# Attention probabilities transposed by DMA instead of by TensorE, in an eight-core block of attention and quantised FFN

## The reference

```
x = x + attn(layernorm(x))
x = x + ffn(layernorm(x))

attn: qkv = x @ w_qkv.T, reshaped to (N, 3, 16 heads, 128)
      att = softmax(einsum('bnid,bnjd->bnij', q, k) * 128**-0.5)
      out = einsum('bnij,bnjd->bnid', att, v)
      out.transpose(0, 2, 1, 3).reshape(B, N, 2048) @ w_proj.T
ffn:  fake_quant(relu(fake_quant(x) @ fake_quant(kernel) + fake_quant(bias)))
```

## Time and profile before

| | us |
|---|---|
| three runs, median (lowest, highest) | 635.04 (634.66, 636.46) |
| the profiled execution, its own time | 635.95 |
| span of its slowest core, core 5 | 634.3 |
| spans of the other cores | 631.6 to 633.4 |
| PE busy on core 5 | 606.1 (96%) |
| DVE / ACT busy on core 5 | 407.9 (64%) / 266.6 (42%) |

### The profile page before, as it was taken

The page is one execution under the profiler, slowest core; times in us unless marked ns, Lnnn a source line. Parts: engine busy times, 40 slices in busy tenths (PEclk is TensorE's granted clock), DMA queues, the critical chain, the costliest instruction groups (busy, mean ns, idle before and its releaser), DMA issues.

```text
span 634.3 us, 9870 instructions; the slowest of 8 cores (631.6 to 634.3 us)
## 1 busy us (share of the span) xinstructions
PE 606.1 (96%) x3468; PEld 304.6 (48%) x3468; DVE 407.9 (64%) x685; ACT 266.6 (42%) x491; POOL 34.7 (5%) x68
## 2 busy tenths in 40 slices
PE   6768999999999999999999999999999999999993
PEld 6634444444444444444444455555555444444442
DVE  3745888777778768761001346787787654888557
ACT  2763333443333344330010465767877422653331
POOL 0000100000100100001120000000000000000000
PEclk9999999999999999999999999999999999999998
DMA  8997899889999999758996672384433494062313
GB/s 236 261 217 221 139 237 219 174 190 195 190 230 185 228 232 194 177 102 150 154 157 102 120 168 78 101 246 121 133 94 61 157 285 136 30 196 106 102 66 133
DMA packets 54114, 103.48 MB, mean 163 GB/s; under 512 B 35633, under 2 KB 35633, under 8 KB 50225
## 3 DMA queue, kind: packets, MB, share of 16 engines
q0 software_dynamic: 9216, 33.56, 33.4%
q1 hardware_dynamic: 42674, 60.90, 31.7%
q10 hardware_dynamic: 2176, 8.39, 3.9%
HBM read 111.21 MB, written 16.79 MB: 202 GB/s over the span
## 4 chain that ended last, share of the span: by engine, by line
PE 89%; DMA 6%; DVE 2%; issue 1%; SPq 1%; ACT 1%; DVEq 0%; ACTq 0%
PE pF L832 50%; PE pF L937 17%; PE pF L914 17%; DMA xbuf<-x_att 6%; PE pF L871 1%; PE pF L895 1%; PE pH L881 1%; PE pF L872 1%; SPq L219 1%; PE pF L956 1%; PE pF L850 1%; DVE cols L514 0%; DVE xr L640 0%; DVEq L214 0%; DVE xr L807 0%
## 5 line engine op out<-in xcount | busy, mean ns | idle before, releaser
L832 PE MATMUL pF<-aT,wqb 128*128 128x512 bf16 x1504 | 327.1, 379 | 5.0 <-DMA wqb<-wqkv 5.0
L832 PEld LDWEIGHTS pF<-aT,wqb 128*128 128x128 bf16 x1504 | 146.4, 98 | 179.3 <-issue 5.4
L914 PE MATMUL pF<-wpq,qT 128*128 128x512 bf16 x512 | 119.6, 379 | 0.0
L937 PE MATMUL pF<-kq,xqT 128*128 128x512 bf16 x496 | 107.2, 379 | 1.2 <-DVE xr L640 1.2
L937 PEld LDWEIGHTS pF<-kq,xqT 128*128 128x128 bf16 x496 | 48.5, 98 | 59.9 <-issue 1.7
L914 PEld LDWEIGHTS pF<-wpq,qT 128*128 128x128 bf16 x512 | 47.8, 98 | 47.2
L385 ACT ACTIVATE wkz<-wkf 128x2048 f32<-128x2048 f32 x16 | 59.1, 3691 | 21.0 <-DVE wkf L607 21.0
L395 ACT ACTIVATE Ebuf<-pF,cols 128x128 bf16<-128x128 f32 x128 | 45.4, 368 | 24.6 <-DVE cols L621 24.5
L541 DVE CAST vT<-pF 128x512 bf16<-128x512 f32 x16 | 11.0, 689 | 62.7 <-PE pF L832 62.7
L685 DVE SCALAR_TENSOR_TENSOR tt<-pF,cols,bqb 128x512 f32<-128x512 f32 x31 | 23.2, 749 | 33.0 <-PE pF L937 33.0
L320 POOL DMA_DIRECT2D wqb<-wqkv x48 | 26.0, 543 | 298.7 <-PE pF L832 244.0
(11 more groups left out here) (79 smaller groups left out, 533.4 us busy)
## 6 DMA issues: line engine op xcount, KB each, us to landing
wqb<-wqkv POOLq DMA_DIRECT2D x48, 512.0 KB, 8.1
wkf<-wk SPq DMA_DIRECT2D x16, 1024.0 KB, 8.4
xbuf<-x_att SPq DMA_DIRECT2D x8, 1024.0 KB, 19.9
kq_spill<-kqr SPq DMA_DIRECT2D x16, 512.0 KB, 5.9
wpq<-wp POOLq DMA_DIRECT2D x16, 512.0 KB, 9.6
xr<-x_res ACTq DMA_DIRECT2D x8, 1024.0 KB, 6.7
kq<-kq_spill SPq DMA_DIRECT2D x4, 2048.0 KB, 11.1
out<-xr SPq DMA_DIRECT2D x7, 1024.0 KB, 4.2
```

Of the source, the lines that this page charges most:

```text
L832: mm = tn.matmul(pF[QBANK[j]][:, :], wqb[e % NW][:, 128 * c:128 * (c + 1)], aT[:, 8192 * h + 512 * c: 8192 * h + 512 * (c + 1)], start=(c ...
L914: mm = tn.matmul(pF[SLOTB[f % 3]][:, :], sT[:, 2048 * b + 128 * m: 2048 * b + 128 * (m + 1)], wpq[u][:, 512 * m:512 * (m + 1)], start=(m = ...
L937: mm = tn.matmul(pF[y % 4][:, :], xqT[:, 2048 * k + 128 * c: 2048 * k + 128 * (c + 1)], w[:, c, :, :], start=(c == 0), stop=(c == NC - 1))
```

## The change

The four PE transposes of each group and the ACT copy behind them are removed. In their place SP issues one transposing DMA per group, `e_transpose(g)`, from `Ebuf[g % 3]` to `aTT[g % 3]`; both have three buffers instead of two. It waits for `vNm` (the scaled probabilities) and for `av(g - 3)`, which has then read its `aTT`. `av(g)` waits for the DMA's semaphore `eT{g % 3}` instead of `sAT`, and `exps(g)` for the DMA of group g - 3 instead of the PE transpose of g - 2. Because SP works in order, its list is rewritten: the 32 new entries stand in the order of g, and `v_transpose`, `kq_load(0)` and `l_transpose(0..2)` are placed between them. The matmuls that warm PE up at the start read a tile of their own, `zero`, instead of `aTT[0]`.

```diff
     Ebuf = [A(f"Ebuf{i}", [128, 512], BF16, offset=204800 + 1024 * i)
-            for i in range(2)]
-    aTT = [A(f"aTT{i}", [128, 512], BF16, offset=206848 + 1024 * i)
-           for i in range(2)]
+            for i in range(3)]
+    aTT = [A(f"aTT{i}", [128, 512], BF16, offset=207872 + 1024 * i)
+           for i in range(3)]
+    zero = A("zero", [128, 128], BF16, offset=204800)
...
+            def e_transpose(g):
+
+                sync.wait_ge(S_("vNm"), g + 1)
+                if g >= 3:
+                    sync.wait_ge(S_("tO"), g - 2)
+                inc(sync.dma_start_transpose(
+                    aTT[g % 3].rearrange("p (j n) -> p j n", j=4),
+                    Ebuf[g % 3][:, :]), f"eT{g % 3}", 16)
...
-            for b in range(5):
-                v_transpose(b)
-            kq_load(0)
-            l_transpose(0)
-            v_transpose(5)
-            v_transpose(6)
-            l_transpose(1)
-            v_transpose(7)
-            l_transpose(2)
+            v_transpose(0)
+            v_transpose(1)
+            for g in range(NG):
+                e_transpose(g)
+                if g % 4 == 2 and 2 <= g // 4 + 1 < NT:
+                    v_transpose(g // 4 + 1)
+                if g == 8:
+                    kq_load(0)
+                if g in (17, 23, 29):
+                    l_transpose((g - 17) // 6)
...
             def exps(g):
                 s.wait_ge(S_("vMx"), g + 1)
-                if g >= 2:
-                    s.wait_ge(S_("tA"), g - 1)
+                if g >= 3:
+                    s.wait_ge(S_(f"eT{g % 3}"), 16 * (g // 3))
...
-                if 1 <= sl and sl - 1 < NG:
-                    att_evac(sl - 1)
...
             def av(g):
-                tn.wait_ge(S_("sAT"), g + 1)
+                tn.wait_ge(S_(f"eT{g % 3}"), 16 * (g // 3 + 1))
...
-                    if half == 0 and 1 <= sl <= NG:
-                        a_transp(sl - 1)
```

More of the change, by code:

```diff
@@ L390, in exps @@
                 s.wait_ge(S_("vMx"), g + 1)
-                if g >= 2:
-                    s.wait_ge(S_("tA"), g - 1)
+                if g >= 3:
+                    s.wait_ge(S_(f"eT{g % 3}"), 16 * (g // 3))
                 for j in range(4):
                     cs = slice(128 * j, 128 * (j + 1))
-                    i = s.activation(Ebuf[g % 2][:, cs], pF[3 + g % 2][:, cs],
+                    i = s.activation(Ebuf[g % 3][:, cs], pF[3 + g % 2][:, cs],
                                      AF.Exp, bias=cc(C_NM[g % 2] + j),
@@ L406, in xres_load @@
                         "p (h c) -> p h c", h=2)), f"xrL{b}", 16)
[L408 to L412, removed]
             def st_evac(g):
@@ L630, in a_norm @@
                 wt(v, h)
-                e3 = Ebuf[g % 2].rearrange("p (j n) -> p j n", j=4)
+                e3 = Ebuf[g % 3].rearrange("p (j n) -> p j n", j=4)
                 rb = cc(C_RD[g % 2], 4).unsqueeze(2).broadcast_to([128, 4, 128])
@@ L703, in _ @@
             inc(v.memset(cc(C_NMG), -MAGIC), "vNmg")
-            inc(v.memset(aTT[0][:, 0:128], 0.0), "vZ")
+            inc(v.memset(zero[:, :], 0.0), "vZ")
             stats(0)
@@ L896, in av @@
                                    V8[(g // 4) % 2][:, c0:c0 + 128],
-                                   aTT[g % 2][:, cs], start=True, stop=True)
+                                   aTT[g % 3][:, cs], start=True, stop=True)
                 inc(mm, "tO")
@@ L965, in warm @@
                 for i in range(n):
-                    tn.matmul(pF[5][:, 0:128], aTT[0][:, 0:128],
-                              aTT[0][:, 0:128], start=True, stop=True)
+                    tn.matmul(pF[5][:, 0:128], zero[:, :],
+                              zero[:, :], start=True, stop=True)
             tn.wait_ge(S_("vZ"), 1)
```

## The result

The changed kernel is slower: 648.81 us as the median of four runs (644.26 to 655.9) against 635.11 (634.66 to 636.46), a ratio of 1.018 (95% interval 1.012 to 1.024). Times are medians of all executions, while the ratios and their intervals leave out those in which half of the chip's cores ran at a lower clock, and those more than 1.5% over the kernel's fastest, which here is 655.9 and may be no more than this kernel's own scatter. The forecast was 628.3, with 626.8 to 632.5 as its range. The profiled execution took 644.26 us.

The account below looks back on a forecast made before the run. PE was taken to bound the kernel: 635.95 us profiled, less 7.2 for the transposes, plus 0.2 (group 9) and 0.3 (group 3), gives 629.25; against the runs' median the forecast is 628.3 us, range 626.8 to 632.5.

Parts of the forecast that it names:

- The removed work: Attention slots on PE: dropping four transposes saves 0.225 us per group, 7.2 us over 32 groups, giving slots of 4.12 us.
- The small DMA alone: One 128 x 512 transposing DMA, undisturbed: lands after 2.1 us (bounds 2.1 to 3.7) and holds SP 0.4 us.
- the moved steps: SP's list: v_transpose, l_transpose and the other moved entries cost nothing; v_transpose has 16 us of cover for a 3.7 us landing.
- sharing cost 3.2 us there: Core 1 transpose beside a residual load: landed after 6.9 us instead of 3.7, so a small one lands at 5.3, inside cover.
- group 3: Wait before av(3), its DMA beside a residual load and the wpq loads: taken as 0.3 us, bounds 0 to 1.5.
- `kq_load(0)` and group 9: Wait before av(9), its small DMA queued behind the 2 MB kq_load(0): taken as 0.2 us, bounds 0 to 1.7.
- late in more places: Rival: residual loads and v_transpose entries each delay one group past cover, three to five costing about 1 us; 630-633 us, chance 0.12.
- The slower rival: Rival: small transposes land as slowly as the slowest large ones in every slot, slower above 8.6 us; 637 or 674 us, chance 0.09.

Follow-up runs that it names:

- hybrid5_kq: Changed kernel with groups 0-4 transposed by PE, v_transpose(2..7) one group earlier, kq_load(0) behind group 31, l_transposes behind groups 19, 24, 29: 630.21 us, ratio 0.993.
- v_late: Kernel before the change, with v_transpose(2..7) made to wait so each starts within a microsecond of residual load b - 1: 634.87 us, ratio 1.001.
- v_early: Changed kernel with v_transpose(2..7) issued one group earlier on SP, residual loads still on ACT: 647.11 us, ratio 1.012.
- full_kq: Changed kernel, all 32 groups by DMA, with v_transpose one group earlier, kq_load(0) behind group 31, l_transposes behind groups 19, 24, 29: 639.74 us, ratio 1.007.
- no_wp: Changed kernel without POOL's last four wpq loads, zeros written instead: 641.37 us, ratio 1.010.
- xres_sp: Changed kernel with the eight residual loads issued by SP behind the transposing DMA of group 4b + 3, instead of by ACT: 636.94 us, ratio 1.004.

## Why the prediction was wrong

**The removed work: right.** 0.225 us a group and slots of 4.12 us are what the trace shows, and hybrid5_kq gives the whole sum back (27 x 0.223 us between the first and the last `av`). The Trainium skill's price for a PE transpose (TensorE: Matmul & The Clock Gate, Part 4: PE-mode transpose, about 275 ns) does not hold in this kernel as the cost of one: 108 transposes less gave 6.0 us, 56 ns each.

**The small DMA alone: right.** 2.3 us to land against 2.1. SP's 1.18 us against 0.4 was wrong by a factor of three and cost nothing, as hybrid5_kq shows.

**The step that failed is the moved steps.** The prediction priced `v_transpose(b)` by its cover only ("16 us of cover for 3.7 us") and said of all the moved entries "All of these cost nothing". It did not ask what else is on the DMA engines at the new moment. One group later on SP is the slot of the residual load, and the two start within 1 us of each other in 42 of 48 pairs. The new place alone does this: on core 7 group 10 is scaled at 402.90, its DMA issued at 403.03 and `v_transpose(3)` right behind it at 404.31, so `kq_load(0)` does not hold it up. That load, moved to group 8, was still under way (it landed at 406.0), and the transposes of this place are the slowest, 9.5 to 16.4 us against 7.7 to 11.3 elsewhere; that the third transfer is why is not shown.

The 3.7 us were a price from a place where the DMA engines were idle. v_late shows the collision by itself. v_early takes it away but at `v_transpose(3)`, which there does stand behind `kq_load(0)`, and hybrid5_kq and full_kq take that away too. Measured, this term is 7.2 us after `av(4)` as the mean of the cores and 10.6 on the worst, where the sum had 0.2 for group 9 and nothing else.

**The second failed term is "sharing cost 3.2 us there".** It came from one place, core 1, where I read the load's packets in the window as two transfers that ran side by side. They hardly did: the residual load was issued at 417.29, 7 us before the transpose (424.23); the transpose's first packet came at 426.37, and only the load's last 33 packets, up to 427.15, were left then.

Against an undisturbed transpose 1.0 of the 3.1 us lie before the first packet and 0.6 in the packets, which ran from 426.37 to 429.10; the last 1.5 lie between the last packet and the landing, when the load had landed (427.7), and what held it there is open. No row of the kernel before shows the two in each other's middle. A transpose that starts with a load takes 7.7 to 16.4 us, not 6.9.

The same row let group 3 pass as covered. That group was taken at 0.3 us, with a bound of 1.5 from loads that land when they did before, but they land later too (on core 7 the fourth `wpq` load after 14.0 us, where it took 8.7). Measured, groups 1 to 4 lost 3.6 to 8.4 us. no_wp shows that none of it comes without the `wpq` loads, and xres_sp that group 3's part goes too when residual load 0 leaves ACT's queue. I had also left groups 1 and 2 out, though the same `wpq` loads run beside them.

**`kq_load(0)` and group 9:** forecast 0 to 1.7 us at `av(9)`, measured 0.0 to 2.2 by core (core 7: 0.2). That term was nearly right in itself, and blind to what stands behind.

**The clock was not in the sum.** Behind the eight longest waits of the changed kernel (3.2 to 6.3 us) the slot has a granted clock of 0.63 to 0.74 on average, part of it at the lower level, and takes 1.4 to 2.3 us more than 4.12 (1.5 on core 7 behind the wait before `av(11)`). In v_early it is up to 2.9.

**The rivals.** The first one, "late in more places", was the right one in kind: it named residual loads and `v_transpose` entries. It was priced at 630 to 633, about 1 us a place, and refused with "6.9 us, for a DMA four times as large, is still under 7.9", the same row again. The lost time is 6.9 to 18.6 us by core. The slower rival needed a median landing over 8.6 us and was wrong: the median is 4.2, and no core's is higher than 4.4. I gave slower 0.09, because I asked only whether *every* group could be late and not whether a few could be very late.

## What to carry to other kernels

Where a DMA takes the place of an engine's work, price its landing beside what other queues move in that very microsecond, not from a row in which it ran alone, and do the same for each entry that is moved to make room. Small packets, transposing ones above all, should not start with another queue's load: put both on one queue, or keep them apart (a lead of 1.2 to 2.1 us was enough for the transpose here, 4.5 us and more in hybrid5_kq, where nothing is lost), or leave the work on the engine in the few slots where this can't be done. When each of many steps has its own cover, one late one costs its excess in full and the clock behind it, so sum over the worst places, and on the worst core, before the average.

## What the runs showed of the hardware

- A transposing DMA of 512 KB and a 1 MB load from memory on another queue, started within 1 us of each other, took 7.7 to 16.4 and 6.4 to 16.3 us in the changed kernel, and 8.0 to 11.5 and 7.4 to 10.9 in v_late; 6 us apart, in the kernel before, they take 3.6 to 5.5 and 5.0 to 8.2 (b = 2 to 7 without the pair at `kq_load(0)`). For microseconds they move 14 to 101 GB/s together, with packets under way in most slices in the changed kernel and in half of them in v_late. The size of the packets is the larger part for the copy (8.2 us in 256-byte pieces, 3.2 in 4 KB, 9.8 transposed). The Trainium skill says that DMAs of all issuing engines run on the same 16 engines and interleave (DMA: Bandwidth & Descriptors, Issuing engines are not separate DMA queues); here packets of both queues do lie in one window, 4836 of queue 1 and 272 of queue 10 in 404 to 422 us, but the sum of their rates is not kept. What goes on inside the engines no run here shows.
- 1 MB loads on the same queue as the transposes do not do this: in xres_sp nothing is lost at groups 7, 11, 15 and 27, and `v_transpose(2)` to `(7)` land after 3.7 to 7.2 us.
- A transposing DMA holds SP for 1.18 us with 128 x 512 and for 1.7 with 128 x 2048, so most of it is fixed.
- In PE's wait of 6.3 us before `av(11)` on core 7 its granted clock went from 1.00 to 0.50. It was 0.50 in the first part of the slot behind the wait and 1.00 in the last, and the slot took 5.64 us instead of 4.12.

What stays open: whether the `wpq` loads, which come from POOL's queue and are converted from float32 to bf16 on the way, slow the small DMAs by the same effect as the residual loads or by another, or simply by their amount, since no run moved them to SP's queue. The runs show only that both do. It is also open why some cores and executions lose two or three times as much as others.
